# The last pair of a batched two-map residual kernel: rows in another order, stored in blocks, 16 channels computed twice

## The reference

```python
W = L0_cond_weights[itok_B_0_15]            # one of 16 maps, 128 x 128, for each entry
x = x + einsum('bct,bcd->bdt', x, W)
w = L1_cond_weights[itok_B_0_31]            # one of 32 maps
x = x + einsum('bct,bcd->bdt', x, w) + bias[itok_B_0_31] transposed
return x                                    # 128 x 128 x 2048, fp32
```

## Time and profile before

| | |
|---|---|
| median of 3 runs | 642.05 us (641.68 to 642.21) |
| the profiled execution, its own time | 642.29 us |
| its span in the trace | 640.4 us |
| PE (TensorE) busy | 538.4 us, 84% |
| DVE (VectorE) busy | 329.2 us, 51% |
| ACT (ScalarE) busy | 333.5 us, 52% |
| POOL (GpSimd) busy | 124.2 us, 19% |
| mean transfer rate over the span | 424 GB/s |

### The profile page before, as it was taken

The page is one execution under the profiler, slowest core; times in us unless marked ns, Lnnn a source line. Parts: engine busy times, 40 slices in busy tenths (PEclk is TensorE's granted clock), DMA queues, the critical chain, the costliest instruction groups (busy, mean ns, idle before and its releaser), DMA issues.

```text
span 640.4 us, 6061 instructions
## 1 busy us (share of the span) xinstructions
PE 538.4 (84%) x2308; PEld 234.3 (37%) x2308; DVE 329.2 (51%) x259; ACT 333.5 (52%) x385; POOL 124.2 (19%) x263
## 2 busy tenths in 40 slices
PE   1899999999889889888898898888988988988860
PEld 0344444444334333333333333333333333433320
DVE  0266666666554455455545554555455445545550
ACT  0366666666555465455554654555555545545550
POOL 2322222222122122121221221211212212112000
PEclk9999999999999999999999999999999999999995
DMA  8999999999999999999999999999999999999996
GB/s 363 433 415 427 431 432 426 431 433 428 432 433 427 432 434 427 431 434 427 432 434 426 433 435 426 432 433 428 433 431 428 433 431 430 431 433 428 434 429 262
DMA packets 18931, 271.82 MB, mean 424 GB/s; under 512 B 2241, under 2 KB 2274, under 8 KB 2274
## 3 DMA queue, kind: packets, MB, share of 16 engines
q1 hardware_dynamic: 9504, 137.37, 50.3%
q10 hardware_dynamic: 9410, 134.26, 49.0%
HBM read 137.40 MB, written 134.22 MB: 424 GB/s over the span
## 4 chain that ended last, share of the span: by engine, by line
DMA 64%; PE 29%; DVE 3%; POOLq 0%; ACT 0%; issue 0%; DVEq 0%; POOL 0%; SPq 0%; ACTq 0%
DMA out_dram<-xt 40%; PE acc L159 25%; DMA xt<-in_x_dram 23%; PE acc L154 4%; DMA w_sb<-in_w_dram 1%; DVE xt L224 1%; DVE xt L226 1%; DVEq L39 0%; ACT L246 0%; POOLq L126 0%; POOLq L129 0%; POOL map0T L136 0%; POOL map L137 0%; ACT both L247 0%; ACT both L246 0%
## 5 line engine op out<-in xcount | busy, mean ns | idle before, releaser
L159 PE MATMUL acc<-xt,both 64*128 64x512 f32 x2048 | 472.5, 603 | 67.9 <-DMA xt<-in_x_dram 65.7
L251 ACT ACTIVATE xt<-acc,bias_of 64x1024 f32<-64x1024 f32 x256 | 283.7, 1108 | 270.1 <-PE acc L159 267.7
L159 PEld LDWEIGHTS acc<-xt,both 64*128 64x128 f32 x2048 | 189.8, 188 | 319.0 <-issue 211.5
L224 DVE TENSOR_SCALAR xt<-acc,bias_of 64x1024 f32<-64x1024 f32 x128 | 163.3, 1276 | 278.2 <-PE acc L159 278.2
L226 DVE TENSOR_SCALAR xt<-acc,bias_of 64x1024 f32<-64x1024 f32 x128 | 165.0, 1289 | 1.9
L136 POOL TENSOR_TENSOR map0T<-w0T_sb,ident 128x128 f32<-128x128 f32 x128 | 65.6, 513 | 465.8 <-PE acc L154 454.0
L154 PE MATMUL acc<-map,map0T 128*128 128x256 f32 x256 | 73.3, 409 | 1.2 <-POOL map L137 1.2
L137 POOL TENSOR_TENSOR map<-w_sb,ident 128x128 f32<-128x128 f32 x128 | 65.7, 513 | 0.0
L154 PEld LDWEIGHTS acc<-map,map0T 128*128 128x128 f32 x256 | 43.9, 191 | 53.0 <-issue 36.7
L247 ACT ACTIVATE both<-acc 64x256 f32<-64x256 f32 x64 | 24.3, 380 | 0.8
L246 ACT ACTIVATE both<-acc 64x256 f32<-64x256 f32 x64 | 24.2, 377 | 0.8
(11 more groups left out here) (4 smaller groups left out, 0.4 us busy)
## 6 DMA issues: line engine op xcount, KB each, us to landing
xt<-in_x_dram SPq DMA_DIRECT2D x64, 2048.0 KB, 24.5
out_dram<-xt ACTq DMA_DIRECT2D x64, 2048.0 KB, 42.9
w_sb<-in_w_dram SPq DMA_DIRECT2D x1, 2048.0 KB, 9.4
w0T_sb<-in_w0T_dram SPq DMA_DIRECT2D x1, 1024.0 KB, 4.8
cond_sb<-in_conds_dram ACTq DMA_DIRECT2D x1, 1.0 KB
bias_sb<-in_bias_dram ACTq DMA_DIRECT2D x1, 16.0 KB, 9.4
cond_rep<-in_conds_dram ACTq DMA_DIRECT2D x1, 16.0 KB, 10.8
```

The lines of the kernel that those rows point to most:

```text
L159: return nc.tensor.matmul(acc[:, j * CHUNK:(j + 1) * CHUNK], both[k * HC:(k + 1) * HC, buf, u, :], xt[k * HC:(k + 1) * HC, slot, u * T + j ...
L224: nc.vector.tensor_scalar(xt[0:HC, q % SLOTS, a:a + HALF], acc0[0:HC, a:a + HALF], bias_of[0:HC, 2 * q:2 * q + 1], None, ALU.add)
L251: return nc.scalar.activation(xt[HC:C, q % SLOTS, v * T + a:v * T + a + HALF], acc1[v * HC:(v + 1) * HC, a:a + HALF], ACT.Identity, bias=b ...
```

## The change

The tile shapes of the first 63 pairs and all that is issued for them stay. For pair 63 the output channels stand in another order on the partitions: the columns of the combined map are put down in another order when ScalarE copies it out of PSUM (four copies instead of two), and the bias with them. The results go to a tile of their own, `last`, so that the input stays in `xt`. Partition `64k + 32h + 4e + r` of `last` holds what was row `16r + 8h + e` of entry `k`. The store of `last` is not one DMA of 128 rows but several of 16, 12 and 32 rows, two from ScalarE and four from GpSimd, and leaves out the block `k = 0, e = 4` (`AWAY`), 8 rows of 16 KB. Ahead of each of GpSimd's groups a small copy of five rows, `aside`, is issued.

The 16 channels of that block are computed again by eight matmuls that write 16 rows of `acc0`, after both halves of pair 63 have been emptied. VectorE adds their bias into `spare`, and ScalarE stores `spare` with two DMAs of 16 rows of 4 KB. The biases of pair 63, in the new order and for the 16 channels, are made before the loop by two more matmuls and four more VectorE copies.

```diff
+    AWAY = 4
+    last_rows = out_pairs[PAIRS - 1, :, :].rearrange("(k r h e) f -> k h e r f", k=2, r=4, h=2)
+    away_rows = out[B - 2, :, :].rearrange("(m e u) t -> e m u t", e=8, u=2)[AWAY, :, :, :]
...
+        biasT_last = sb("biasT_last", [S1, C])
+        biasT_away = sb("biasT_away", [S1, 16])
+        bias_last = sb("bias_last", [C, 2])
+        bias_away = sb("bias_away", [16, 2])
+        last = sb("last", [C, 2 * T])
+        spare = sb("spare", [C, T])
+        aside = sb("aside", [5, 2, 32], int32)
...
+        both_away = sb("both_away", [HC, 2, 16])
...
+            for h in range(2):
+                nc.gpsimd.dma_start(aside[:, :, h * 16:(h + 1) * 16],
+                                    row[0:5, 0:64].rearrange("p (a b) -> p a b", a=2)[:, :, 0:16]).then_inc(aside_filled[h], LOAD)
+                if h == 0:
+                    pool.wait_ge(hi_out[SLOTS - 1], 2 * TURNS)
+                at = 32 * h
+                nc.gpsimd.dma_start(last_rows[0, h, AWAY + 1:8, :, :],
+                                    last[at + 4 * AWAY + 4:at + 32, :]).then_inc(mid_stored[h], LOAD)
+                nc.gpsimd.dma_start(last_rows[1, h, :, :, :],
+                                    last[HC + at:HC + at + 32, :]).then_inc(high_stored[h], LOAD)
...
+            nc.tensor.matmul(acc0[:, CHUNK:CHUNK + 2], biasT_last[:, :], onehot[:, B - 2:B], start=True, stop=True).then_inc(picked_last, 1)
+            nc.tensor.matmul(acc1[0:16, CHUNK:CHUNK + 2], biasT_away[:, :], onehot[:, B - 2:B], start=True, stop=True).then_inc(picked_away, 1)
...
+            pe.wait_ge(bias_last_ready, 1)
+            pe.wait_ge(bias_away_ready, 1)
...
+            pe.wait_ge(lo_out[SLOTS - 1], 2 * TURNS)
+            pe.wait_ge(hi_out[SLOTS - 1], 2 * TURNS)
+            for j in range(T // CHUNK):
+                for u in range(2):
+                    away = nc.tensor.matmul(acc0[0:16, j * CHUNK:(j + 1) * CHUNK], both_away[:, u, :],
+                                            xt[0:HC, SLOTS - 1, u * T + j * CHUNK:u * T + (j + 1) * CHUNK],
+                                            start=u == 0, stop=u == 1)
+            away.then_inc(away_done, 1)
...
-            nc.vector.tensor_copy(biasT[:, :, :], acc0[0:S1, 0:C].rearrange("s (i u) -> s u i", u=2)).then_inc(biasT_ready, 1)
+            nc.vector.tensor_copy(biasT[:, :, :], acc0[0:S1, 0:C].rearrange("s (i u) -> s u i", u=2))
+            nc.vector.tensor_copy(biasT_last[:, :].rearrange("c (u s r) -> c u r s", u=2, r=4),
+                                  acc0[0:S1, 0:C].rearrange("c (r s u) -> c u r s", u=2, r=4))
+            nc.vector.tensor_copy(biasT_away[:, :].rearrange("c (m u) -> c m u", u=2),
+                                  acc0[0:S1, 0:C].rearrange("c (m e u) -> c e m u", e=8, u=2)[:, AWAY, :, :]).then_inc(biasT_ready, 1)
...
+            dve.wait_ge(picked_last, 1)
+            nc.vector.tensor_copy(bias_last[:, :], acc0[:, CHUNK:CHUNK + 2]).then_inc(bias_last_ready, 1)
+            dve.wait_ge(picked_away, 1)
+            nc.vector.tensor_copy(bias_away[:, :], acc1[0:16, CHUNK:CHUNK + 2]).then_inc(bias_away_ready, 1)
...
-            def even_out(q, a):
-                nc.vector.tensor_scalar(xt[0:HC, q % SLOTS, a:a + HALF], acc0[0:HC, a:a + HALF],
-                                        bias_of[0:HC, 2 * q:2 * q + 1], None, ALU.add)
-                return nc.vector.tensor_scalar(xt[0:HC, q % SLOTS, T + a:T + a + HALF], acc0[HC:C, a:a + HALF],
-                                               bias_of[HC:C, 2 * q:2 * q + 1], None, ALU.add)
+            def even_out(to, bias, a):
+                nc.vector.tensor_scalar(to[0:HC, a:a + HALF], acc0[0:HC, a:a + HALF], bias[0:HC, :], None, ALU.add)
+                return nc.vector.tensor_scalar(to[0:HC, T + a:T + a + HALF], acc0[HC:C, a:a + HALF], bias[HC:C, :], None, ALU.add)
...
             for q in range(PAIRS):
+                to, bias = xt[:, q % SLOTS, :], bias_of[:, 2 * q:2 * q + 1]
+                if q == PAIRS - 1:
+                    dve.wait_ge(bias_last_ready, 1)
+                    to, bias = last[:, :], bias_last[:, 0:1]
                 dve.wait_ge(lo_done0, q + 1)
-                even_out(q, 0).then_inc(lo_out[q % SLOTS], 1)
+                even_out(to, bias, 0).then_inc(lo_out[q % SLOTS], 1)
                 dve.wait_ge(hi_done0, q + 1)
-                even_out(q, HALF).then_inc(hi_out[q % SLOTS], 1)
+                even_out(to, bias, HALF).then_inc(hi_out[q % SLOTS], 1)
+            dve.wait_ge(bias_away_ready, 1)
+            dve.wait_ge(away_done, 1)
+            nc.vector.tensor_scalar(spare[0:16, 0:HALF], acc0[0:16, 0:HALF], bias_away[:, 0:1], None, ALU.add)
+            nc.vector.tensor_scalar(spare[HC:HC + 16, HALF:T], acc0[0:16, HALF:T], bias_away[:, 0:1], None,
+                                    ALU.add).then_inc(away_out, 1)
...
+                if q == PAIRS - 1:
+                    for k in range(2):
+                        for u in range(2):
+                            nc.scalar.activation(
+                                both[k * HC:(k + 1) * HC, 1, u, :].rearrange("p (v s r) -> p v r s", v=2, r=4),
+                                crossed[k * HC:(k + 1) * HC, u, k, :].rearrange("p (v r s) -> p v r s", v=2, r=4), ACT.Identity)
+                    for u in range(2):
+                        copied = nc.scalar.activation(
+                            both_away[:, u, :].rearrange("p (m v) -> p v m", v=2),
+                            crossed[0:HC, u, 0, :].rearrange("p (v m e) -> p e v m", v=2, e=8)[:, AWAY, :, :], ACT.Identity)
+                    copied.then_inc(both_ready[q % SLOTS], 1)
+                    return
                 nc.scalar.activation(both[0:HC, q % 2, :, :], crossed[0:HC, :, 0, :], ACT.Identity)
                 nc.scalar.activation(both[HC:C, q % 2, :, :], crossed[HC:C, :, 1, :], ACT.Identity).then_inc(both_ready[q % SLOTS], 1)
-            def odd_out(q, v, a):
-                return nc.scalar.activation(xt[HC:C, q % SLOTS, v * T + a:v * T + a + HALF], acc1[v * HC:(v + 1) * HC, a:a + HALF],
-                                            ACT.Identity, bias=bias_of[v * HC:(v + 1) * HC, 2 * q + 1:2 * q + 2])
+            def odd_out(to, bias, v, a):
+                return nc.scalar.activation(to[HC:C, v * T + a:v * T + a + HALF], acc1[v * HC:(v + 1) * HC, a:a + HALF],
+                                            ACT.Identity, bias=bias[v * HC:(v + 1) * HC, :])
...
             copy_maps(0)
             for q in range(PAIRS):
+                to, bias = xt[:, q % SLOTS, :], bias_of[:, 2 * q + 1:2 * q + 2]
+                if q == PAIRS - 1:
+                    act.wait_ge(bias_last_ready, 1)
+                    to, bias = last[:, :], bias_last[:, 1:2]
                 act.wait_ge(lo_done1, q + 1)
-                odd_out(q, 0, 0)
+                odd_out(to, bias, 0, 0)
                 if q < PAIRS - 1:
                     copy_maps(q + 1)
-                odd_out(q, 1, 0).then_inc(lo_out[q % SLOTS], 1)
+                odd_out(to, bias, 1, 0).then_inc(lo_out[q % SLOTS], 1)
                 act.wait_ge(hi_done1, q + 1)
-                odd_out(q, 0, HALF)
-                odd_out(q, 1, HALF).then_inc(hi_out[q % SLOTS], 1)
+                odd_out(to, bias, 0, HALF)
+                odd_out(to, bias, 1, HALF).then_inc(hi_out[q % SLOTS], 1)
                 act.wait_ge(hi_out[q % SLOTS], 2 * (q // SLOTS + 1))
-                act.dma_start(out_pairs[q, :, :], xt[:, q % SLOTS, :]).then_inc(stored[q % SLOTS], LOAD)
+                if q < PAIRS - 1:
+                    act.dma_start(out_pairs[q, :, :], to).then_inc(stored[q % SLOTS], LOAD)
+            for h in range(2):
+                act.dma_start(last_rows[0, h, 0:AWAY, :, :], last[32 * h:32 * h + 4 * AWAY, :]).then_inc(low_stored[h], LOAD)
+            act.wait_ge(away_out, 1)
+            for a in range(2):
+                act.dma_start(away_rows[:, :, a * HALF:(a + 1) * HALF],
+                              spare[a * HC:a * HC + 16, a * HALF:(a + 1) * HALF]).then_inc(away_stored[a], LOAD)
             for q in range(SLOTS):
-                act.wait_ge(stored[q], LOAD * TURNS)
+                act.wait_ge(stored[q], LOAD * (TURNS if q < SLOTS - 1 else TURNS - 1))
+            for h in range(2):
+                act.wait_ge(low_stored[h], LOAD)
+                act.wait_ge(aside_filled[h], LOAD)
+                act.wait_ge(mid_stored[h], LOAD)
+                act.wait_ge(high_stored[h], LOAD)
+                act.wait_ge(away_stored[h], LOAD)
```

More of the change, by code:

```diff
@@ L94, in conditioned_residual_kernel @@
         stored = [sem(f"stored{q}") for q in range(SLOTS)]
+        picked_last = sem("picked_last")
+        picked_away = sem("picked_away")
+        bias_last_ready = sem("bias_last_ready")
+        bias_away_ready = sem("bias_away_ready")
+        away_done = sem("away_done")
+        away_out = sem("away_out")
+        low_stored = [sem(f"low_stored{h}") for h in range(2)]
```

(4 more changed lines are left out.)

## The result

The changed kernel is slower: a median of 644.93 us over 7 runs (643.52 to 646.01) against 642.21 (641.68 to 642.67), a ratio of 1.0035 with a 95% interval of 1.0023 to 1.0047. The forecast was 638.2, its range 637.3 to 642.3: it went the other way. The profiled execution is the fastest of the seven, 643.52 us with a span of 641.6.

The account below looks back on a forecast made before the run. Transfers were taken to bound the kernel, with one engine late at the end; relieving it was to gain 3.9 us, other parts hidden: 642.3 to 638.4 profiled, 638.15 against the median, given as 638.2, range 637.3 to 642.3.

Parts of the forecast that it names:

- What bounds the kernel: Whole span: transfers set the pace at 426 to 431 GB/s; at the end one engine is late by eight rows.
- That the late engine is the one relieved: Last stores: the engine left without its eight rows is the late one, so its lag of 4.2 to 4.8 us goes.
- Rival C: Last stores: the late engine isn't the one relieved, or blocks spread otherwise; time about 642.05 to 642.7; chance 0.23 together.
- The parts at nothing: Before the loop and in the last pairs: bias work, longer copies and more DMA issues are hidden, taken as 0.
- The recomputation: After the last eviction at 622.85: eight matmul calls, 16 records of 0.45 us, 7.1 us, until 630.0.
- rival D: End of kernel: recomputation at 1.2 GHz throughout, 13.4 us of matmuls, time 642.4 to 644.3; chance 0.10.
- The issues of the two stores: After the evictions of the recomputed rows: two issues on ScalarE of 0.34 us each, done at 633.3.
- The order of the tail: End of kernel: recomputed rows land at 633.9 to 635.8, by the time the rings are empty at 635.2 to 635.8.

Follow-up runs that it names:

- the other block: Changed kernel without the recomputation, block 5 left out instead of block 4, GpSimd's small copy six rows long: 642.75 us, ratio 1.0009 to the kernel before.
- the shifted copy: Changed kernel without the recomputation, block 4 not written, GpSimd's first small copy four rows instead of five: 642.8 us, ratio 1.0003 to the kernel before.
- the kernel with all blocks: Changed kernel with block 4 stored from `last` with the blocks below it and nothing computed again: 642.82 us, ratio 1.0003 to the kernel before.
- full columns: Changed kernel with the recomputation on all 128 output columns instead of 16, the other 112 unused: 645.13 us, ratio 1.0035 to the kernel before.
- the version without unused work: Changed kernel with one wait moved, so the low columns' recomputation no longer waits for the high halves' eviction: 639.03 us, ratio 0.9952 to the kernel before.
- block 5's rows from SP: Changed kernel without recomputation; SP stores block 5's eight rows in two DMAs of four, block 4 not written: 643.03 us, ratio 1.0004 to the kernel before.

## Why the prediction was wrong, point by point

**What bounds the kernel:** right. The lone engine, late by one store's share, was read correctly out of the earlier trace rows, and its relief was sized at 3.6 to 4.8 us; without the recomputation it is 3.8.

**That the late engine is the one relieved:** right, with 0.23 against it. The rows could not settle it; the kernel without the recomputation did, and the other block and the shifted copy bear it out. Rival C falls. It leaned on the Trainium skill, "DMA: Bandwidth & Descriptors", section "Latency and other measured facts", by which engines 7 and 15 are usually the slower ones; in the kernel without the recomputation only block 4's rows are gone, and every other engine is through by 635.6, those two among them.

**The parts at nothing** (bias work, copies, blocks, GpSimd's issues): right, by the kernel with all blocks. GpSimd's DMAs were out 2.8 us after the wait, 0.55 us each.

**The recomputation:** here it failed. The term of 7.1 us in the sum measured 11.6 us in the profiled run. The price at the full rate was right, 7.04 us with the gap filled, but 2.4 GHz wasn't granted for 9.4 us of it. The sentence that failed is "from nothing to 6.7 us of the block run at half speed, and up to 3.3 us are lost". It took the return to 2.4 GHz from the start of the kernel, where the matmuls run on both halves of the array. These run on one, and the clock never came back: 9.4 us in the changed kernel and 14 us with full columns. So what came is rival D, which had a chance of 0.10. Its sum, 13.4 us of matmuls and 642.4 to 644.3 us, is close to the median of 644.93, which lies 0.6 us above it; the profiled run has 11.6 us because the clock fell 2.2 us into the block. The argument against D, that the 6.7 us seen at the start are short of the 8.2 us it takes, rested on the same comparison.

**The issues of the two stores:** 1.40 us instead of 0.68, since a DMA of this shape costs ScalarE 0.70 us. That is 0.7 us, paid in the changed kernel, where these stores end last.

**The order of the tail:** the engines were put through at 635.2 to 635.8 and the recomputed rows landed at 633.9 to 635.8, so the sum had 0 to 1.9 us of slack for a longer block. 4.5 us more of matmuls made 4.5 us more of span.

The runs show that matmuls on half the array didn't bring the clock up again, where those on both halves did at the start. Whether the halves decide it or something else wasn't tried, since no run has matmuls on both halves after a gap at the end. That the gap cost the clock is shown: filling it, or starting the block without one, kept 2.4 GHz for the whole 7.04 us.

## What to carry to other kernels

Read the last microseconds of a transfer-bound kernel in fine windows: a DMA share of 0.06 is one engine still at work, and its last share can be taken away. What is put in its place must end before the other engines do, and matmuls behind a gap are to be priced at 1.2 GHz for their whole length unless a row shows the clock coming back under that same shape of work. The cheapest cure for such a gap is to move a wait, so that the part of the new work that is ready starts right behind the old.

## What the runs showed of the hardware

- One DMA engine ends late: 4.2 to 4.8 us at the end of 640, with plain loads and stores from SP and ScalarE. The stretch came back in every kernel in which it kept its rows, on three chips. By the rule for GpSimd's DMAs it is number 4. Why it is slower no run here tells.
- The granted clock fell 2.8 us after the last matmul in the kernel before, and in the changed kernel 2.2 us after matmuls had resumed behind 2.76 us of idle time. It then stayed at 1.2 GHz under 9.4 and 14 us of uninterrupted matmuls on 64 array rows, and it stayed at 2.4 GHz under 7.04 us of the same matmuls when there was no gap. The time from the last matmul to the fall is not fixed: 1.2 us in the version without unused work (627.8 to 628.9; PEclk 0.73 over 628 to 630) and 4.4 us with block 5's rows from SP (620.9 to 625.3; 0.67 over 624 to 628). So the same gap of 2.8 us can cost the clock before the next matmuls or after they have begun.
- An issue on ScalarE took 0.34 us for a store of 128 rows and 0.7 to 1.2 us for the small ones, on SP 1.05 us for 16 pieces of 512 B, on GpSimd 0.55 us.
- Four engines reading rows of 16 KB out of four neighbouring partitions took 1.4 to 3.1 us a row with block 5 and 1.1 to 4.9 us with block 4, against 0.61 us.
